# A decoder layer's mixer: masked products in two buffers, and the weighing of a finished group moved behind level 0 and the gate projection

## The chip, the cores and the metric

The kernel runs on one core of a Trainium2 chip. The metric is device time in microseconds of one execution, the median over the runs. Engines are named as in the profile: PE (TensorE, matmuls), PEld (its weight loads), DVE (VectorE), ACT (ScalarE), POOL (GpSimd), SP (SyncE, which issues DMAs).

## The reference

One decoder layer over 32 sequences of 100 tokens with 256 channels, in float32, with three stages, each with a residual: a recurrent mixer, cross attention, and experts. Only the mixer is touched:

```python
def step(S, inp):
    q_t, k_t, v_t, w_t = inp
    kv = k_t[..., :, None] * v_t[..., None, :]
    o_t = jnp.einsum('bhk,bhkv->bhv', q_t, S + u[None, :, :, None] * kv)
    S = jnp.exp(w_t)[..., None] * S + kv
    return (S, o_t)
...
o = (o - mean) / jnp.sqrt(var + EPS)
o = o.reshape(B, T, Hh * V) * gn_weight + gn_bias
o = o * jax.nn.silu(g)
return o @ W_o.T
```

Here q, k, v, w and g are projections of the normalised input mixed with its shifted self, w = -exp(...), and there are 4 heads with keys of 32 and values of 64.

## The kernel before

The mixer (`stage_mixer`) works on 8 groups of 4 sequences. The recurrence is not stepped: for each sequence and head a 100 x 100 matrix of weights between tokens, `attn`, is built in 8 levels. Level 0 gives the diagonal. Levels 1 to 7 give the blocks whose size doubles with each level; between levels q and k are multiplied by decay products (`decay_q`, `decay_k`, L512 and L528). On PE, `level` (L723) multiplies k by `q_heads` into `bank_l`; on ACT, `heads` (L394) lays out `q_heads` for the next level; on DVE, `collect` (L535) copies the products from `bank_l` into `attn` under a mask (L542 for level 0, L562, L554, L555 and L552 for the others). Entries that no mask takes stay zero, from one memset on POOL (L282).

When all levels of a group are collected, PE's `weigh` (L744) multiplies `attn` with the values into the two banks `bank_t`. DVE takes the statistics of each head of the result (`head_stats`, L565, per bank; `head_moments`, L571), POOL the reciprocal root (`head_norm`), DVE centres and scales (`head_scale`, L577), PE turns it (`turn_out`), ACT applies weight and bias, POOL multiplies with the gate, PE projects (`project_out`), and DVE adds to the residual.

Groups overlap: the body for group g does the levels of g, the end of g-1 (from the weighing on) and, with the pieces of `front`, the beginning of g+1 (mixing and projections; piece 7 is g's own gate projection). Each engine runs its own list of such steps in the order in which it is written, with semaphores between engines; there is no planner. Groups 0, 1, 6 and 7 are written out, 2 to 5 are a loop of two turns with two bodies each. On DVE, in a body's step s = 0, stand the first bank's statistics of g-1, the collecting of level 0, the second bank's statistics and the moments; in step 1 `decay_q`, `decay_k`, the collecting of level 1, `head_scale` and the gate. On PE a body begins with the weighing of g-1.

`attn` is one buffer. So the collecting of level 0 of g waits until the weighing of g-1 is done (`o_summed`):

```python
dve.wait_ge(level_summed, g * LEVELS * G + j + 1)
after(dve, o_summed, 2 * g)
```

and `level` lets the second half of level 0 wait for the copies of the first half, since two banks are used in turn.

Of the kernel before, what the change touches and what calls it, by code (L numbers as in the profile page):

```python
# [26 lines left out]
BATCH, T, D = 32, 100, 256  # L27
# [41 lines left out]
def stage_mixer(nc, w, x, x1, slot_rows, out, filled):  # L69
# [9 lines left out]
    with ExitStack() as ctx:  # L79
# [44 lines left out]
        decay = sb("decay", [128, 2, G, TP])  # L124
        total = sb("total", [128, 2, G * TP // 2])
        q_heads = sb("q_heads", [128, 2, RH, G, T])
        attn = sb("attn", [T, G, RH, T])
        val = sb("val", [T, 2, G, D])
        tanh_g = sb("tanh_g", [128, CC, GT])
        half_g = sb("half_g", [128, CC, GT])  # L130
# [126 lines left out]
        def _(pool):  # L257
# [21 lines left out]
            norm(0)  # L279
            pool.memset(q_heads[:, 0], 0.0).then_inc(consts, 1)  # L280
            pool.memset(q_heads[:, 1], 0.0).then_inc(consts, 1)
            pool.memset(attn[:], 0.0).then_inc(consts, 1)  # L282
            pool.memset(total[:], 1.0).then_inc(consts, 1)
            pool.wait_ge(consts, CONSTS)

# [24 lines left out]
            for i in range(BRANCHES):  # L310
                mix(0, i)
            norm(1)

            def body(g, p, more):
                first = isinstance(g, int) and g == 0
# [134 lines left out]
        def _(dve):  # L450
# [81 lines left out]
                dve.tensor_tensor(kv[:, :, 0], kv[:, :, 0], tv[:, :, 1:2].to_broadcast([128, nseg, half]),  # L532
                                  ALU.mult).then_inc(k_decayed, 1)

            def collect(g, lv):  # L535

                if lv == 0:
                    for j in range(G):
                        dve.wait_ge(level_summed, g * LEVELS * G + j + 1)
                        after(dve, o_summed, 2 * g)  # L540
                        dve.sem_inc(waited, 1)
                        dve.copy_predicated(attn[:, j], diagonal[:].unsqueeze(1).to_broadcast([T, RH, T]),  # L542
                                            bank_l[j % 2][0:T, 0:GT].rearrange("p (h t) -> p h t", h=RH)
                                            ).then_inc(attn_done, 1)
                    return
                for i in range(2):
                    dve.wait_ge(level_summed, (g * LEVELS + lv) * G + 2 * i + 2)
                    cols = COLS[lv]
                    src = bank_l[i][0:T, 0:8 * cols].rearrange("p (n c) -> p n c", n=8)
                    dst = attn[:, 2 * i:2 * i + 2].rearrange("p b h t -> p (b h) t")  # L550
                    if lv == LEVELS - 1:
                        dve.tensor_copy(dst[0:64, :, 64:T], src[0:64]).then_inc(attn_done, 1)  # L552
                    elif lv == LEVELS - 2:
                        dve.tensor_copy(dst[0:32, :, 32:64], src[0:32, :, 0:32]).then_inc(attn_done, 1)  # L554
                        dve.tensor_copy(dst[64:96, :, 96:T], src[64:96, :, 32:36]).then_inc(attn_done, 1)  # L555
                    else:
                        half = 1 << (lv - 1)
                        nseg = cols // half
                        to = dst[:, :, 0:nseg * 2 * half].rearrange("p n (s two h) -> p n s two h", two=2, h=half)
                        mask = masks[:, lv - 1, 0:cols].rearrange("p (s h) -> p s h", h=half)  # L560
                        dve.sem_inc(waited, 1)
                        dve.copy_predicated(to[:, :, :, 1], mask.unsqueeze(1).to_broadcast([T, 8, nseg, half]),  # L562
                                            src.rearrange("p n (s h) -> p n s h", h=half)).then_inc(attn_done, 1)
# [43 lines left out]
            def body(g, p, more):  # L607
                first = isinstance(g, int) and g == 0
                for s in range(LEVELS):
                    if s == 5 and two_more(g):  # L610
                        norm_stats(g + 2)
                    if 1 <= s < LEVELS - 1:
                        decay_q(g, p, s + 1)
                        decay_k(g, p, s + 1)
                    if s == 0 and not first:
                        head_stats(g - 1, 0)
                    collect(g, s)
                    if s == 0 and not first:
                        head_stats(g - 1, 1)
                        head_moments(g - 1)  # L620
                    if s == 1 and not first:
                        head_scale(g - 1)
                    if s == 7 and two_more(g):
                        front(g + 2, p, 1)
                    if s == 1 and not first:
                        front(g, p, 7)
                    if more and 1 < s < 7:
                        front(g + 1, 1 - p, s)
                    if 5 <= s <= 6 and not first:
                        residual(g - 1, s - 5)  # L630
# [9 lines left out]
        def _(pe):  # L640
# [103 lines left out]
            def weigh(g, p):  # L744
# [3 lines left out]
                for i in range(2):  # L748
                    for j in (2 * i, 2 * i + 1):
                        for h in range(RH):  # L750
                            mm = pe.matmul(bank_t[i][0:T, (j % 2) * D + h * RV:(j % 2) * D + (h + 1) * RV],
                                           attn[:, j, h, :], val[:, p, j, h * RV:(h + 1) * RV], start=True, stop=True)
                    mm.then_inc(o_summed, 1)

            def turn_out(g):
# [25 lines left out]

            def body(g, p, more):
                first = isinstance(g, int) and g == 0
                if not first:
                    weigh(g - 1, 1 - p)
                for s in range(LEVELS):
                    if s == 0 and not first:
                        level(g, p, 0, (0, 1))
                        front(g, 7)
                        level(g, p, 0, (2, 3))  # L790
                    else:
                        level(g, p, s)
                    if s == 2 and not first:
# [1339 lines left out]
```

## Time and profile before

| what | value |
|---|---|
| median of 3 runs | 1441.59 us |
| lowest and highest | 1439.81 and 1442.03 us |
| the profiled execution | 1454.23 us |
| its span, first to last instruction | 1452.4 us |
| its mean granted TensorE clock | 0.967 |
| mixer, from the start to its last residual add | about 416 us |

The profile is one execution, with its own time; the span is what the instructions cover of it. A timeline row gives the start and the length in us of instructions of the same kind merged into one row, with their count, and in brackets the idle time of the engine before them and what ended it. A PE row counts two passes for each float32 matmul.

### The profile page before, as it was taken

Reading aid. Unit: us, or ns where it says so; the run is one execution under the profiler, and the core shown is the slowest. Engines: PE = TensorE matmul, PEld = TensorE weight load, DVE = VectorE, ACT = ScalarE, POOL = GpSimd, SP = SyncE. Lnnn points to the kernel's source line nnn. Section 1 sums busy time; section 2 is a strip of 40 time slices with the busy share of each in tenths; the row PEclk is TensorE's granted clock in tenths of the full one; section 3 lists DMA queues with packets and bytes.
Section 4 is the critical chain, followed back from the end, with each engine's and each line's share of the span. In section 5 each row is a group of like instructions: output and inputs, shape, how many; then the busy total and the mean of one; then the engine's idle time right before and its main releaser. Section 6 shows DMA issues by size and latency. Waiting matters only on the chain.

```text
span 1452.4 us, 30935 instructions
## 1 busy us (share of the span) xinstructions
PE 1316.8 (91%) x9852; PEld 889.5 (61%) x9853; DVE 934.3 (64%) x1964; ACT 622.5 (43%) x1519; POOL 746.1 (51%) x1080
## 2 busy tenths in 40 slices
PE   5789998999749999999999999999988999999996
PEld 3456655666535666666666666666655566666664
DVE  2587787777614888888888888888884322222221
ACT  2455544554313555555555555555543221211221
POOL 5234443243144678777787777877754322222222
PEclk9999999999757999999999999999999999999998
DMA  4996000000026554545544545545532322222221
GB/s 143 281 318 176 1 1 1 0 1 1 1 64 88 106 118 120 122 123 124 124 101 120 122 124 126 117 121 125 117 85 59 56 45 44 47 45 46 44 44 22
DMA packets 152749, 127.80 MB, mean 88 GB/s; under 512 B 41630, under 2 KB 145510, under 8 KB 152614
## 3 DMA queue, kind: packets, MB, share of 16 engines
q1 hardware_dynamic: 140310, 112.02, 31.3%
q0 software_dynamic: 12304, 14.10, 6.3%
q8 instruction: 71, 1.16, 0.4%
q14 instruction: 64, 0.52, 0.1%
HBM read 35.90 MB, written 44.83 MB: 56 GB/s over the span
## 4 chain that ended last, share of the span: by engine, by line
PE 56%; DVE 8%; issue 3%; ACT 2%; DMA 1%; SPq 0%; another core or an unknown queue 0%; POOL 0%; DVEq 0%; ACTq 0%; POOLq 0%
PE bank_st L1948 10%; PE bank_v L1966 7%; PE bank_s L1780 6%; PE bank_v L1768 6%; PE bank_o L1810 4%; PE bank_st L1790 4%; DVE neg_raw L1469 4%; PE bank_m L1743 4%; PE bank_s L1948 3%; PE bank_m L1832 2%; PE bank_st L1799 2%; DVE bank_st L1480 2%; PE bank_o L1957 2%; PE bank_v L1758 1%; PE bank_m L1820 1%
## 5 line engine op out<-in xcount | busy, mean ns | idle before, releaser
L1469 DVE TENSOR_REDUCE neg_raw<-bank_s 100x2 f32<-100x722 f32 x256 | 229.4, 896 | 32.1 <-PE bank_s L1780 30.2
L1316 ACT ACTIVATE prob<-bank_st 120x400 f32<-120x400 f32 (+1 forms) x384 | 166.2, 513 | 159.4 <-PE bank_st L1799 159.4
L1256 POOL DMA_INDIRECT out<-result,target x57 | 88.4, 1550 | 234.4 <-DVE result L1686 186.0
L1480 DVE TENSOR_SCALAR bank_st<-bank_st 121x1200 f32<-121x1200 f32 x128 | 180.3, 1408 | 1.2 <-PE bank_st L1790 0.8
L1681 DVE TENSOR_TENSOR hidden<-silu,bank_st 128x512 f32<-128x512 f32 x57 | 39.2, 688 | 192.7 <-PE bank_st L1948 192.7
L1948 PE MATMUL bank_st<-expert_w,rows_t 128*128 x344 | 159.3, 599 | 0.7 <-issue 0.5
L409 ACT ACTIVATE q_heads<-q 32x192 f32<-32x192 f32 (+3 forms) x224 | 82.7, 369 | 140.8 <-DVE q L521 136.4
L1780 PE MATMUL bank_s<-k_st,q_st 96*128 96x361 bf16 x512 | 124.1, 324 | 15.5 <-DVE neg_raw L1469 10.1
L1155 POOL TENSOR_TENSOR neg_diag<-xident_b,neg_max 100x400 bf16<-100x400 bf16 x128 | 109.4, 855 | 47.6 <-DVE neg_max L1474 47.0
L741 PE MATMUL bank_l<-q_heads,k 128*100 128x192 f32 (+4 forms) x512 | 114.9, 366 | 18.7 <-ACT q_heads L409 7.3
L293 POOL TENSOR_TENSOR mixed<-part,xn_t 128x400 f32<-128x400 f32 x80 | 84.4, 1080 | 82.0 <-DVE part L462 81.9
L1425 ACT ACTIVATE hidden_t<-bank_o 128x512 f32<-128x512 f32 x57 | 34.0, 597 | 196.5 <-PE bank_o L1957 190.3
L741 PEld LDWEIGHTS bank_l<-q_heads,k 128*100 128x100 f32 x512 | 81.5, 172 | 51.9 <-issue 14.0
L1790 PE MATMUL bank_st<-q_st,k_st 96*128 96x100 bf16 x1536 | 108.6, 209 | 5.0 <-ACT prob L1316 0.6
L1790 PEld LDWEIGHTS bank_st<-q_st,k_st 96*128 96x128 bf16 x1536 | 83.0, 98 | 43.4 <-ACT prob L1316 28.7
L1966 PE MATMUL bank_v<-residual,hidden_t 128*128 x456 | 108.0, 380 | 1.0 <-ACT hidden_t L1425 0.9
L1948 PEld LDWEIGHTS bank_st<-expert_w,rows_t 128*128 128x128 f32 x344 | 63.6, 192 | 71.9 <-issue 71.7
L1743 PE MATMUL bank_m<-kv,xw_k 96*128 96x361 f32 x256 | 93.6, 490 | 10.9 <-DMA kv<-in_ctx_t 10.2
L1768 PE MATMUL bank_v<-xw_v,kv 96*120 96x256 f32 (+1 forms) x384 | 98.5, 394 | 1.4 <-ACT xval L1334 0.7
L1810 PE MATMUL bank_o<-prob,xval 120*32 120x100 f32 (+1 forms) x3072 | 93.7, 255 | 0.0
L1799 PE MATMUL bank_st<-neg_diag,xones_b 100*128 100x400 bf16 x384 | 87.3, 336 | 5.1 <-DVE bank_st L1480 5.1
L1966 PEld LDWEIGHTS bank_v<-residual,hidden_t 128*128 128x128 f32 x456 | 82.3, 190 | 10.8 <-issue 2.0
(231 smaller groups left out, 2545.8 us busy)
## 6 DMA issues: line engine op xcount, KB each, us to landing
k_st<-k_part SPq DMA_DIRECT2D x384, 90.2 KB
slot_rows<-empty SPq DMA_DIRECT2D x9, 2967.0 KB, 26.3
q_st<-q_part SPq DMA_DIRECT2D x192, 50.0 KB
kv<-in_ctx_t SPq DMA_DIRECT2D x32, 270.8 KB
expert_w<-in_w SPq DMA_DIRECT2D x16, 512.0 KB
rows<-slot_rows SPq DMA_DIRECT2D x57, 129.0 KB
residual<-in_w SPq DMA_DIRECT2D x16, 256.0 KB
residual<-in_x SPq DMA_DIRECT2D x8, 400.0 KB
```

The source lines that it names most:

```text
L741: pe.matmul(bank[0:T, at:at + RH * cols], k[:, p, j, 0:T], q_heads[:, lv % 2, :, j, 0:cols], start=True, stop=True).then_inc(level_summed, 1)
L1316: act.activation(prob[0:KEYS[c], t % 2, c], bank_st[0:KEYS[c], c, 0:4 * T], ACT.Exp).then_inc(exp_done, 1)
L1469: dve.tensor_reduce(neg_raw[:, h:h + 2], bank_s[0:T, :, 0:S], AX.X, ALU.max, negate=True).then_inc(max_done, 1)
L1480: dve.tensor_scalar(tile, tile, CLAMP, -CLAMP, ALU.min, ALU.max).then_inc(clipped, 1)
L1743: mm = pe.matmul(bank_m[:, 0:S], w_k[:, i, c * 128:(c + 1) * 128], kv[:, p, i], start=(i == 0), stop=(i == 1))
L1768: mm = pe.matmul(bank_v[0:KEYS[c], (c % 2) * D:(c % 2 + 1) * D], kv[:, p, i, KEY0[c]:KEY0[c] + KEYS[c]], w_v[:, i], start=(i == 0), stop=( ...
L1780: mm = pe.matmul(bank_s[0:WIDE, i, 0:S], q_st[r][:, h * T:h * T + WIDE], k_st[r][:, h * S:(h + 1) * S], start=True, stop=True)
L1790: mm = pe.matmul(bank_st[0:WIDE, c, j * T:(j + 1) * T], k_st[r][:, at:at + WIDE], q_st[r][:, h * T:(h + 1) * T], start=(j == 0), stop=Fals ...
L1799: pe.matmul(bank_st[0:WIDE, c, 0:4 * T], ones_b[:], neg_diag[:, t % 2].rearrange("p j t -> p (j t)"), start=False, stop=True, skip_group_c ...
L1810: mm = pe.matmul(bank_o[32 * j:32 * j + 32, t * T:(t + 1) * T], val[0:KEYS[c], p, c, 17 * (4 * t + j):17 * (4 * t + j) + 32], prob[0:KEYS[ ...
L1948: mm = pe.matmul(dst, rows_t[:, u, c], w1_of[:, bass.ds(expert, 1), c, half * F:(half + 1) * F].rearrange("p o f -> p (o f)"), start=(c == ...
L1966: mm = pe.matmul(ebank_y[:, 0:D], hidden_t[:, u, f], w2_of[:, bass.ds(expert, 1), f].rearrange("p o d -> p (o d)"), start=(f == 0), stop=( ...
```

## The change

`attn` gets a second buffer; the parity p of the group selects it in the collecting and the weighing. POOL zeroes the second buffer later than the first, behind the first group's mixing and the second group's norm; DVE waits for that once, in group 1. The collecting of level 0 now waits for the weighing of g-2. On DVE both banks' statistics stand behind all of the collecting of level 0. On PE the weighing stands behind level 0, whose halves enclose the gate projection.

```diff
-        attn = sb("attn", [T, G, RH, T])
+        attn = sb("attn", [T, 2, G, RH, T])
...
-            pool.memset(attn[:], 0.0).then_inc(consts, 1)
+            pool.memset(attn[:, 0], 0.0).then_inc(consts, 1)
...
             norm(1)
+            pool.memset(attn[:, 1], 0.0).then_inc(consts, 1)
...
-            def collect(g, lv):
+            def collect(g, p, lv, batches=range(G)):
...
-                        after(dve, o_summed, 2 * g)
+                        after(dve, o_summed, 2 * (g - 1))
...
-                        dve.copy_predicated(attn[:, j], diagonal[:].unsqueeze(1).to_broadcast([T, RH, T]),
+                        dve.copy_predicated(attn[:, p, j], diagonal[:].unsqueeze(1).to_broadcast([T, RH, T]),
...
+                    if isinstance(g, int) and g == 1 and s == 0:
+                        dve.wait_ge(consts, CONSTS + 1)
                     if s == 0 and not first:
+                        collect(g, p, 0)
                         head_stats(g - 1, 0)
-                    collect(g, s)
-                    if s == 0 and not first:
                         head_stats(g - 1, 1)
                         head_moments(g - 1)
+                    else:
+                        collect(g, p, s)
...
-                                           attn[:, j, h, :], val[:, p, j, h * RV:(h + 1) * RV], start=True, stop=True)
+                                           attn[:, p, j, h, :], val[:, p, j, h * RV:(h + 1) * RV], start=True, stop=True)
...
-                if not first:
-                    weigh(g - 1, 1 - p)
                 for s in range(LEVELS):
                     if s == 0 and not first:
                         level(g, p, 0, (0, 1))
                         front(g, 7)
                         level(g, p, 0, (2, 3))
+                        weigh(g - 1, 1 - p)
                     else:
                         level(g, p, s)
```

PE at the start of body 1, before. L673 is the turning of the normalised input (the end of the body before), L751 the weighing, L741 the levels (400 columns: level 0; 200: levels 1 and 2), L644 with w_g the gate projection, L680 the first projection of the next group:

```order
L673 MATMUL bank_f<-ident,xn 128x100 x8
L751 MATMUL bank_t<-val,attn 100x64 x16
L741 MATMUL bank_l<-q_heads,k 100x400 x2
L644 MATMUL bank_f<-mixed,w_g 128x400 x4
L741 MATMUL bank_l<-q_heads,k 100x400 x2
L741 MATMUL bank_l<-q_heads,k 100x200 x4
L680 MATMUL bank_f<-xz,w_x 128x400 x4
```

The same place with the change (its lines are numbered 4 higher):

```order
L677 MATMUL bank_f<-ident,xn 128x100 x8
L745 MATMUL bank_l<-q_heads,k 100x400 x2
L648 MATMUL bank_f<-mixed,w_g 128x400 x4
L745 MATMUL bank_l<-q_heads,k 100x400 x2
L755 MATMUL bank_t<-val,attn 100x64 x16
L745 MATMUL bank_l<-q_heads,k 100x200 x4
L684 MATMUL bank_f<-xz,w_x 128x400 x4
```

The 16 matmuls of the weighing have moved from ahead of level 0 to behind it, ahead of level 1.

DVE at the start of body 1, before: L568 the statistics, L542 the collecting of level 0, L575 the moments, L521 to L532 the decays, L562 the collecting of level 1:

```order
L568 BN_STATS gn_stats<-bank_t 100x6 x8
L542 COPY_PREDICATED attn<-diagonal,bank_l 100x400 x4
L568 BN_STATS gn_stats<-bank_t 100x6 x8
L575 BN_AGGR gn_mv<-gn_stats 100x2 x16
L521 TENSOR_TENSOR q<-q,decay 128x256
L525 TENSOR_TENSOR total<-decay 128x256
L532 TENSOR_TENSOR k<-k,decay 128x256
L562 COPY_PREDICATED attn<-masks,bank_l 100x400 x2
```

With the change (lines numbered 1 higher):

```order
L543 COPY_PREDICATED attn<-diagonal,bank_l 100x400 x4
L569 BN_STATS gn_stats<-bank_t 100x6 x16
L576 BN_AGGR gn_mv<-gn_stats 100x2 x16
L522 TENSOR_TENSOR q<-q,decay 128x256
L526 TENSOR_TENSOR total<-decay 128x256
L533 TENSOR_TENSOR k<-k,decay 128x256
L563 COPY_PREDICATED attn<-masks,bank_l 100x400 x2
```

The first 8 statistics have moved behind the four copies; all 16 now stand between the copies and the decays.

## Rows read from the trace of the kernel before

**Rows 1.** The page: busy time, share of the span, instructions of each engine.

```profile
PE 1316.8 (91%) x9852; PEld 889.5 (61%) x9853; DVE 934.3 (64%) x1964; ACT 622.5 (43%) x1519; POOL 746.1 (51%) x1080
```

**Rows 2.** Busy time in a stretch from weighing to weighing; then clock, DMA share, GB/s.

```profile
267.00:311.81 44.81, 41.31 (x197) 28.65 (x195) 35.98 (x99) 23.27 (x54) 17.99 (x18) 1.00 0.00 0
```

**Rows 3.** PE's waits from 86 to 356 us: total us, times, longest.

```profile
PE bank_f L644 <- POOL mixed L293: 8.2, 6, 1.4
PE bank_t L761 <- DVE normed L589: 5.5, 10, 0.9
PE bank_l L741 <- ACT q_heads L409: 4.0, 4, 1.1
PE bank_l L741 <- DVE attn L542: 2.3, 7, 1.1
```

**Rows 4.** Timeline of PE at the boundary of group 6: start, length, line, operation.

```profile
311.81 3.04 PE L751 MATMUL bank_t<-val,attn 100*100 100x64 f32 x32
314.68 1.54 PE L741 MATMUL bank_l<-q_heads,k 128*100 128x400 f32 x4
316.06 2.85 PE L644 MATMUL bank_f<-mixed,w_g 128*128 128x400 f32 x8
318.74 1.51 PE L741 MATMUL bank_l<-q_heads,k 128*100 128x400 f32 x4
320.51 1.57 PE L741 MATMUL bank_l<-q_heads,k 128*100 128x200 f32 x8 [0.26 <-DVE attn L542]
...
325.50 1.73 PE L741 MATMUL bank_l<-q_heads,k 128*100 128x200 f32 x8 [0.74 <-DVE attn L562]
```

**Rows 5.** Timeline of DVE at the same boundary.

```profile
316.47 1.14 DVE L568 BATCH_NORM_STATS2 gn_stats<-bank_t 100x6 f32<-100x64 f32 x8
...
319.76 1.27 DVE L542 COPY_PREDICATED attn<-diagonal,bank_l 100x400 f32<-100x400 int32 x2 [1.16 <-PE bank_l L741]
320.93 1.14 DVE L568 BATCH_NORM_STATS2 gn_stats<-bank_t 100x6 f32<-100x64 f32 x8
...
323.30 0.39 DVE L521 TENSOR_TENSOR q<-q,decay 128x256 f32<-128x256 f32 x1
```

**Rows 6.** Timeline of ACT at the same boundary.

```profile
310.32 0.60 ACT L382 ACTIVATE val<-bank_f 100x512 f32<-100x512 f32 x1 [0.90 <-PE bank_f L651]
310.81 2.57 ACT L409 ACTIVATE q_heads<-q,bonus 32x400 f32<-32x400 f32 x4
```

**Rows 7.** Timeline of ACT at groups 1, 2 and 5.

```profile
85.30 2.56 ACT L409 ACTIVATE q_heads<-q,bonus 32x400 f32<-32x400 f32 x4
...
129.92 2.56 ACT L409 ACTIVATE q_heads<-q,bonus 32x400 f32<-32x400 f32 x4
...
279.00 1.60 ACT L409 ACTIVATE q_heads<-q 32x200 f32<-32x200 f32 x4 [3.96 <-DVE q L521]
```

**Rows 8.** Timeline of PE at groups 1, 2, 5 and 7.

```profile
89.00 1.54 PE L741 MATMUL bank_l<-q_heads,k 128*100 128x400 f32 x4
...
133.96 1.54 PE L741 MATMUL bank_l<-q_heads,k 128*100 128x400 f32 x4
...
280.82 1.60 PE L741 MATMUL bank_l<-q_heads,k 128*100 128x200 f32 x8 [0.92 <-ACT q_heads L409]
...
356.59 3.04 PE L751 MATMUL bank_t<-val,attn 100*100 100x64 f32 x32 [0.54 <-DVE attn L552]
```

**Rows 9.** Timeline of DVE at group 7.

```profile
358.25 1.15 DVE L568 BATCH_NORM_STATS2 gn_stats<-bank_t 100x6 f32<-100x64 f32 x8 [1.72 <-PE bank_t L751]
```

**Rows 10.** Timeline of POOL in the first 65 us.

```profile
12.31 1.43 POOL L282 MEMSET attn<- 100x1600 f32 x1
...
64.30 3.90 POOL L293 TENSOR_TENSOR mixed<-part,xn_t 128x400 f32<-128x400 f32 x4 [17.37 <-DVE part L462]
```

**Rows 11.** Timeline of DVE at group 4, where the loop turns.

```profile
227.33 1.15 DVE L568 BATCH_NORM_STATS2 gn_stats<-bank_t 100x6 f32<-100x64 f32 x8 [1.89 <-issue]
```

**Rows 12.** Timeline of PE: the last group's weighing.

```profile
393.01 4.92 PE L751 MATMUL bank_t<-val,attn 100*100 100x64 f32 x32 [0.71 <-DVE attn L552]
```

More of the change, by code:

```diff
@@ L533, in decay_k @@
                                   ALU.mult).then_inc(k_decayed, 1)
-            def collect(g, lv):
+            def collect(g, p, lv, batches=range(G)):
                 if lv == 0:
-                    for j in range(G):
+                    for j in batches:
                         dve.wait_ge(level_summed, g * LEVELS * G + j + 1)
-                        after(dve, o_summed, 2 * g)
+                        after(dve, o_summed, 2 * (g - 1))
                         dve.sem_inc(waited, 1)
-                        dve.copy_predicated(attn[:, j], diagonal[:].unsqueeze(1).to_broadcast([T, RH, T]),
+                        dve.copy_predicated(attn[:, p, j], diagonal[:].unsqueeze(1).to_broadcast([T, RH, T]),
                                             bank_l[j % 2][0:T, 0:GT].rearrange("p (h t) -> p h t", h=RH)
@@ L549, in collect @@
                     src = bank_l[i][0:T, 0:8 * cols].rearrange("p (n c) -> p n c", n=8)
-                    dst = attn[:, 2 * i:2 * i + 2].rearrange("p b h t -> p (b h) t")
+                    dst = attn[:, p, 2 * i:2 * i + 2].rearrange("p b h t -> p (b h) t")
                     if lv == LEVELS - 1:
```

## The prediction

> **What bounds the kernel now.** I read the page first, then the stretches from one weighing to the next, then PE's waits, then the timelines of PE, ACT and DVE around one boundary between groups. On the page PE is busy for 91% of the span [rows 1], so the naive reading is that only PE's work counts. A stretch from one weighing to the next corrects that: it lasts 44.81 us and PE is busy in 41.31 of them, at a granted clock of 1.00 (its 2.4 GHz level) [rows 2]. PE's idle time in six such stretches is four kinds of wait [rows 3]: for POOL's mixed (8.2), for DVE's normed (5.5), for ACT's heads (4.0) and for the level 0 copy of DVE, L542 (2.3), with a smaller one for L562. All lie in the first half of a group, between the weighing and the projection on w_r; behind that projection PE runs without a wait to the group's end. So a group is a fixed PE run plus a chain across engines, and whatever lengthens that chain lengthens the kernel. The mixer comes before a block boundary, so nothing later takes up its delay.
>
> The chain at the boundary of group 6 (body 6) reads: PE weighs from 311.81, starts level 0 at 314.68, the gate projection at 316.06, the second half of level 0 at 318.74 [rows 4]. DVE takes the first bank's statistics at 316.47, waits 1.16 us for level 0, copies from 319.76, starts the second bank's statistics at 320.93, and reaches decay_q at 323.30 [rows 5]. From decay_q on, level 2's heads, the collecting, normed, part and mixed follow in DVE's order, and all PE waits named above hang on them. **decay_q's start is the clock by which the change is to be judged.**
>
> **What is removed and moved: the start of level 0.** The weighing, 2.87 us of PE (314.68 − 311.81), leaves the place ahead of level 0. Level 0 does not start 2.87 us sooner, because it needs all four heads of ACT. Their activations start at 310.81, straight behind the value copy that started at 310.32, and take 2.57 us: they end at 313.38 [rows 6]. From an ACT head's end to PE's first matmul on it took 0.22 us (279.00 + 1.60 = 280.60, PE at 280.82 [rows 7, 8]). So level 0 starts at 313.60, sooner by 1.08 us, and PE idles from 311.81 to 313.60, a new wait of 1.79 us. At group 1 the same sum gives 85.30 + 2.56 + 0.22 = 88.08 against 89.00, 0.92 sooner; at group 2 129.92 + 2.56 + 0.22 = 132.70 against 133.96, 1.26 sooner [rows 7, 8]. Nothing brings the heads forward: ACT's order is untouched.
>
> **What the move puts on the chain: the weighing before the statistics.** Call level 0's start S. Before, the second statistics started at S + 6.25 (320.93 − 314.68). Now PE issues half of level 0 (1.38, from 314.68 to 316.06), the gate projection (2.68, to 318.74), the other half (1.38) and then the weighing (2.88). That the weighing's last bank is readable 0.22 us after its last issue I take from the last group, where nothing covered it: weighing from 356.59, half of it 1.44, first statistics at 358.25 [rows 8, 9]. The second statistics start at S + 1.38 + 2.68 + 1.38 + 2.88 + 0.22 = S + 8.54: later by 2.29 us against S. The last two level 0 copies do leave DVE sooner: their pair starts 1.02 us behind its half of level 0 (319.76 − 318.74) and takes 1.27, so with S = 313.60 it ends at 313.60 + 4.06 + 1.02 + 1.27 = 319.95. But DVE then stands at the first statistics until the weighing has begun (S + 5.44) and its first bank is readable (1.66 later, 358.25 − 356.59), at 320.70, and again at the second until 322.14. From there to decay_q it is 2.37 us as before (323.30 − 320.93): 324.51 in place of 323.30. Behind it are queued the 16 moments, decay_q, decay_k, level 1's collecting and head_scale, and ACT and POOL wait for those.
>
> **Sum.** 2.29 − 1.08 = 1.21 us a group at group 6; 2.29 − 0.92 = 1.37 at group 1, 2.29 − 1.26 = 1.03 at group 2. Groups 1 to 7 weigh their predecessor in the moved place (the eighth weighing, at the end, is untouched): 7 × 1.21 = **8.5 us**. PE's side agrees in sign: the old waits ahead of level 1 (0.26) and level 2 (0.74 [rows 4]) are swallowed at most in part, against 1.79 us new.
>
> **The other edits.** The second zeroing on POOL costs what the first did, 1.43 us, and lies in the 17.37 us that POOL idles before its mixing at 64.30 [rows 10]; uncovered it would cost 1.43, once. DVE's added wait for it comes in group 1, near 90 us, where the zeroing can start at 46.93 (64.30 − 17.37); I take 0 for a wait already fulfilled, and 0.26, the smallest wait of [rows 4], as its upper end. The copies' wait for the weighing of two groups before is long satisfied, and takes nothing away either, since in the old order PE's queue put the weighing ahead of level 0 anyway: what stalled DVE there was PE's position, not the buffer. No DMA is moved. A code-loading pause can shift: DVE shows one of 1.89 us with no releaser where the loop turns [rows 11]; 0 is my value, −1.89 (it goes) and +3.78 (two more) the ends.
>
> A rule speaks for this change. PE's wait for the level 0 copy comes back at every boundary, 7 waits of 2.3 us in all [rows 3]. The Trainium skill, Perfetto Trace Analysis, Optimization Strategy, says that the same gap repeated on the engine that should be saturated can mean too few buffers. By that rule the second attn buffer would remove those 2.3 us and the kernel would come to about 1439.3; the rows say that the gap belongs to the order, since DVE waited for PE [rows 5].
>
> The profiled execution took 1454.23 us, 12.6 more than the median of 1441.59; the sum gives 1462.7 for such an execution and **1450.1 us** for the median. I carry the 8.5 over unchanged.
>
> **Rivals.**
> 1. *Faster: the heads don't hold level 0.* If the heads were ready when PE is free, level 0 would start 2.87 sooner against 2.29 lost: −0.58 a group, −4.1 in seven, **1437.5 us**. It decides at a head start of 2.29 us: the heads would have to end by about 312.2. For it: only PE's order changes, and PE's order was the binding one. Against it: they ended at 313.38 [rows 6], and the value copy ahead of them waits for PE's own projection, so they move with PE.
> 2. *No change: only PE's order is permuted.* DVE's delay is taken up by waits already there (PE waits 8.2 us in six groups for mixed [rows 3]), or PE's 2.3 us of waits for the level 0 copy go and nothing comes in their place: **1439.3 to 1443 us**. Against: mixed is itself behind DVE's part, in DVE's order behind decay_q.
> 3. *Much slower: the clock falls.* Weighing in the last group took 4.92 us where it takes 3.04 at the full level [rows 4, 12], after PE had idled more: the 1.2 GHz level. If each of the 7 new idles brought such a fall, and each cost these 1.88 us, 13.2 come on top: **1463.3 us**. Against: the waits of up to 1.1 us in these groups left it at 1.00 [rows 2, 3]; 1.79 in one piece is new.
>
> The Trainium skill, TensorE: Matmul & The Clock Gate, A second HAM failure mode, says that short idles between groups of matmuls, frequent enough, make the clock swing between its levels; by it rival 3 would come about.
>
> That the change doesn't do what it says is excluded for the order, by the rows of PE and DVE shown with the change.
>
> **How the numbers follow.** Forecast 0.80, rival 1 0.06, rival 2 0.08, rival 3 0.06. The forecast's own span: seven groups at 1.03 to 1.37 give 7.2 to 9.6; with the pause and a microsecond or so of the last group's changing clock it reaches from 1445 to 1456.5. The range is **1444 to 1456.5**: it leaves out rivals 1 and 3 and most of 2, near 2 in 10. A measurement of this kernel tells about 0.2% (2.9 us) from no change. Faster by more than that: rival 1 and a sliver, 0.07. Within: rival 2 and the forecast's lowest corner, 0.09. Slower: 0.84.
>
> **What would show it.** In the profile after: PE stands idle about 1.8 us before each group's first level 0 matmul, released by ACT's q_heads; the wait for L542 almost goes; DVE waits for bank_t before both statistics of a group; and a stretch from one weighing to the next lasts about 46.0 us instead of 44.8. Wrong: stretches no longer than before (the chain had slack), a PE idle of well under a microsecond ahead of level 0 (the heads came sooner), or a granted clock below 1.00 inside groups 1 to 6.

## The result, and the profile after

The changed kernel takes 1447.05 us in the median of 6 runs (1445.81 to 1452.35), the kernel before 1441.07 us (1439.81 to 1442.25, 6 runs). The ratio is 1.0047, with a 95% interval of 1.0030 to 1.0064: slower by about 6.8 us (4.3 to 9.2 by the interval; the medians differ by 6.0), where 8.5 was predicted.

The span of the profiled execution moved the other way, from 1452.4 to 1447.4 us. That comes from the stages behind the mixer, which the edit doesn't touch: from the mixer's last residual add to the span's end it is 1036.6 us before (1452.4 − 415.8), 1025.6 changed (1447.4 − 421.8), and 1024.5 (1437.7 − 413.2) in the run with only the second buffer below. This part took 1024.5 to 1025.6 us in the profiles of the changed kernel and of the first four runs below, and 1035.7 to 1038.2 in those of the last five, whatever their order in the mixer; the profile of the kernel before belongs with the latter. What makes these 11 us is not known. I therefore compare stretches of the mixer, and times only as ratios to the kernel before, run beside it.

The page, busy time by engine, answers to [rows 1]: nothing has changed in the amounts.

```profile
PE 1316.4 (91%) x9852; PEld 890.1 (61%) x9853; DVE 934.8 (65%) x1964; ACT 620.2 (43%) x1519; POOL 746.1 (52%) x1081
```

The stretch from one weighing to the next (group 5 to group 6) answers to [rows 2]: 45.76 us instead of 44.81 with the same PE work, at the same clock of 1.00.

```profile
279.56:325.32 45.76, 41.21 (x196) 28.81 (x195) 36.18 (x100) 23.24 (x53) 17.97 (x18) 1.00 0.00 1
```

PE's waits from 86 to 360 us, against [rows 3]: the wait for ACT's heads grew from 4.0 to 12.2 us (six new waits ahead of level 0, of 1.48 to 1.67 us, make up 9.5 of them), that for the level 0 copy (now L543) fell from 2.3 to 1.5 and stands at one boundary only, that of group 4, where the loop turns, and those for mixed and normed are as they were.

```profile
PE bank_l L745 <- ACT q_heads L410: 12.2, 10, 1.7
PE bank_f L648 <- POOL mixed L293: 8.2, 6, 1.4
PE bank_t L765 <- DVE normed L590: 5.8, 10, 0.9
PE bank_l L745 <- DVE attn L543: 1.5, 1, 1.5
PE bank_l L745 <- DVE attn L563: 1.1, 2, 0.6
```

PE's timeline at the boundary of group 6 (against [rows 4]). Level 0 starts at 319.86 behind an idle time of 1.48 us; the weighing runs from 325.32 behind level 0's second half.

```profile
317.53 0.85 PE L677 MATMUL bank_f<-ident,xn 100*128 100x100 f32 x8
319.86 1.59 PE L745 MATMUL bank_l<-q_heads,k 128*100 128x400 f32 x4 [1.48 <-ACT q_heads L410]
321.29 2.85 PE L648 MATMUL bank_f<-mixed,w_g 128*128 128x400 f32 x8
323.97 1.51 PE L745 MATMUL bank_l<-q_heads,k 128*100 128x400 f32 x4
325.32 2.96 PE L755 MATMUL bank_t<-val,attn 100*100 100x64 f32 x32
328.11 1.55 PE L745 MATMUL bank_l<-q_heads,k 128*100 128x200 f32 x8
...
332.90 1.73 PE L745 MATMUL bank_l<-q_heads,k 128*100 128x200 f32 x8 [0.55 <-DVE attn L563]
```

ACT at the same boundary (against [rows 6]): the heads start right behind the value copy and end at 319.81. PE starts 0.05 later.

```profile
316.75 0.60 ACT L383 ACTIVATE val<-bank_f 100x512 f32<-100x512 f32 x1 [0.91 <-PE bank_f L655]
317.25 2.56 ACT L410 ACTIVATE q_heads<-q,bonus 32x400 f32<-32x400 f32 x4
```

DVE at the same boundary (against [rows 5]). Both banks' statistics wait for the weighing, 0.64 and 0.27 us, and decay_q starts at 330.69. Decay_k (L533) and the scaling of `normed` (L590) follow.

```profile
324.99 1.27 DVE L543 COPY_PREDICATED attn<-diagonal,bank_l 100x400 f32<-100x400 int32 x2 [1.02 <-PE bank_l L745]
326.90 1.15 DVE L569 BATCH_NORM_STATS2 gn_stats<-bank_t 100x6 f32<-100x64 f32 x8 [0.64 <-PE bank_t L755]
328.31 1.15 DVE L569 BATCH_NORM_STATS2 gn_stats<-bank_t 100x6 f32<-100x64 f32 x8 [0.27 <-PE bank_t L755]
...
330.69 0.39 DVE L522 TENSOR_TENSOR q<-q,decay 128x256 f32<-128x256 f32 x1
...
331.37 0.43 DVE L533 TENSOR_TENSOR k<-k,decay 128x256 f32<-128x256 f32 x1
...
334.69 1.27 DVE L590 TENSOR_TENSOR normed<-normed,gn_rstd 100x512 f32<-100x512 f32 x2
```

To compare the two boundaries, take the end of the body before, E, as zero: the instant at which PE's next instruction could issue. Before, it is the start of the weighing, 311.81. After, the transposes that end the body start at 317.53 and take 0.71 to the next issue, as in the runs below where the weighing still follows them: 318.24. Decay_q then starts at E + 11.49 before (323.30 − 311.81) and at E + 12.45 after (330.69 − 318.24): **0.96 us later, and the stretch is 0.95 us longer** (45.76 − 44.81). Seven groups give 6.7 us.

The body of group 5, read in the same way, gives a little more: decay_q at E + 12.53 (284.93 − 272.40) instead of E + 11.49, and 45.84 us from its E to the next instead of 44.81, thus 1.04 and 1.03. From weighing to weighing it is less, because the wait for the heads is 0.08 us shorter at group 6 than at group 5. Seven times 1.03 is 7.2. The ratio allows 4.3 to 9.2 us, so it tells neither of these sums from the forecast of 8.5; only the stretches do, and that 6.7 comes so close to 6.8 is chance.

### The profile page after: what moved, and what is told of

It reads as the page before. It is cut to its first block, busy times and chain, and to the rows that moved or that the text cites. A ratio compares the mean times of both kernels' runs of the same rounds, so it can differ in the third digit from the quotient of the medians.

```text
span 1447.4 us, 30930 instructions
## 1 busy us (share of the span) xinstructions
PE 1316.4 (91%) x9852; PEld 890.1 (61%) x9853; DVE 934.8 (65%) x1964; ACT 620.2 (43%) x1519; POOL 746.1 (52%) x1081
## 3 DMA queue, kind: packets, MB, share of 16 engines
q8 instruction: 71, 1.16, 0.4%
## 4 chain that ended last, share of the span: by engine, by line
PE 61%; issue 3%; ACT 3%; DVE 3%; DMA 1%; SPq 0%; POOL 0%; ACTq 0%; DVEq 0%; POOLq 0%
PE bank_st L1951 10%; PE bank_v L1969 7%; PE bank_v L1771 6%; PE bank_s L1783 6%; PE bank_st L1793 6%; PE bank_m L1746 6%; PE bank_o L1813 5%; PE bank_s L1951 3%; PE bank_st L1802 3%; PE bank_m L1835 2%; PE bank_o L1960 2%; PE bank_v L1761 1%; DVE neg_raw L1472 1%; PE bank_m L1823 1%; ACT heads_t L1332 1%
## 5 line engine op out<-in xcount | busy, mean ns | idle before, releaser
L1793 PE MATMUL bank_st<-q_st,k_st 96*128 96x100 bf16 x1536 | 113.4, 209 | 5.7 <-ACT prob L1319 0.6
```

What stands on the lines that cost most here:

```text
L1793: mm = pe.matmul(bank_st[0:WIDE, c, j * T:(j + 1) * T], k_st[r][:, at:at + WIDE], q_st[r][:, h * T:(h + 1) * T], start=(j == 0), stop=Fals ...
```

## The experiments

Times are ratios to the kernel before, which took 1441.1 us beside the first four runs, 1453.9 beside the next three and 1453.0 beside the last two. Beside each stands the stretch from the weighing of group 5's body to that of group 6's (44.81 before, 45.76 changed). Edits are shown against the kernel named.

**The second buffer alone** (against the changed kernel: PE's and DVE's old order).

```diff
+                if not first:
+                    weigh(g - 1, 1 - p)
...
                         level(g, p, 0, (2, 3))
-                        weigh(g - 1, 1 - p)
...
                     if s == 0 and not first:
-                        collect(g, p, 0)
                         head_stats(g - 1, 0)
+                    collect(g, p, s)
+                    if s == 0 and not first:
                         head_stats(g - 1, 1)
                         head_moments(g - 1)
-                    else:
-                        collect(g, p, s)
```

> Two attn buffers, with PE and DVE in the order of the kernel before. Theory A (the order alone acts; a group's pace is set by when DVE reaches decay_q): ratio to the kernel before 1.000, within 0.001, and 44.8 us from weighing to weighing. Theory B (the one buffer made PE's repeated wait for the level 0 copy): PE's 2.3 us of waits for that copy go, ratio 0.998, 44.5 us a stretch.

Measured: ratio 0.9998 (0.9989 to 1.0007), and a stretch of 44.80 us:

```profile
266.70:311.50 44.80, 41.31 (x196) 28.64 (x194) 35.97 (x99) 23.26 (x54) 17.98 (x18) 1.00 0.00 0
```

PE's waits for the level 0 copy add up to 2.2 us there, against 2.3. The buffer does nothing by itself, and its zeroing costs nothing that shows. Theory B falls: its 0.998 lies outside the interval.

**DVE's new order alone** (against the changed kernel: the weighing back at the start of PE's body).

```diff
+                if not first:
+                    weigh(g - 1, 1 - p)
...
                         level(g, p, 0, (2, 3))
-                        weigh(g - 1, 1 - p)
```

> Two buffers and DVE's new order (all level 0 copies, then both banks' statistics), with the weighing left ahead of level 0 on PE. Theory A: the first bank's statistics (1.06 us) no longer lie in DVE's wait for level 0's second half, so decay_q comes 1.06 us later: 45.9 us a stretch, +7.4 us in seven groups, ratio 1.005, about all that the whole change costs. Rival C (PE's moved weighing is the cause): ratio 1.000 and 44.8 us.

Measured: ratio 1.0044 (1.0031 to 1.0058), 45.85 us a stretch. DVE's timeline at group 6 shows the mechanism: its wait for level 0's second half grows from 1.16 to 2.23 us, since the first statistics no longer fill it, and all 16 statistics stand behind.

```profile
325.71 1.27 DVE L543 COPY_PREDICATED attn<-diagonal,bank_l 100x400 f32<-100x400 int32 x2 [2.23 <-PE bank_l L745]
326.87 2.19 DVE L569 BATCH_NORM_STATS2 gn_stats<-bank_t 100x6 f32<-100x64 f32 x16
...
330.29 0.40 DVE L522 TENSOR_TENSOR q<-q,decay 128x256 f32<-128x256 f32 x1
```

Decay_q at E + 12.54 (330.29 − 317.75). So DVE's reordering alone (on top of the second buffer, which does nothing) costs what the whole change costs. With PE's part of the change two further terms come in that cancel: level 0 starts sooner, and the statistics wait for the weighing.

**The changed kernel with short heads** (in groups 1 to 7 only the first token of each sequence is laid out for level 0, so the kernel leaves out the rest of the diagonal).

```diff
-                    if lv == 0:
+                    if lv == 0 and not (isinstance(g, int) and g == 0):
+                        src, dst = q[rows, p, :, 0:1], q_heads[rows, 0, h, :, 0:1]
+                    elif lv == 0:
                         src, dst = q[rows, p, :, 0:T], q_heads[rows, 0, h]
```

> The changed kernel, where ACT lays out only the first token of each sequence for level 0 in groups 1 to 7 (the diagonal of the others is left out of the computation, with the same number of instructions and semaphores). Theory A: ACT's four level 0 heads shrink from 2.57 us to about 1 and PE's idle of 1.6 us ahead of level 0 goes almost wholly: some 1.4 us less a stretch than the changed kernel, 44.3 us, ratio to before 0.997. If something else held level 0: 45.8 us and 1.005.

Measured: ratio 0.9982 (0.9973 to 0.9991), 44.46 us. ACT's four heads take 1.25 us instead of 2.56, so the saving was 1.31, less than I had guessed. PE, at group 6, waits 0.17 us for them instead of 1.48:

```profile
310.88 1.59 PE L747 MATMUL bank_l<-q_heads,k 128*100 128x400 f32 x4 [0.17 <-ACT q_heads L412]
```

The stretch shrinks by 1.30 us, one for one with the heads.

**The kernel before with the same short heads**, the control (same edit).

> The kernel before with the same shortened level 0 heads, the control. Theory A: the weighing covers the heads there, so nothing changes: 44.8 us, ratio 1.000 within 0.001. Rival (shorter heads help by themselves, by way of ACT's copy of xn_t and DVE's delta behind them): up to 1.4 us a stretch, ratio 0.993.

Measured: ratio 0.9996 (0.9987 to 1.0005), 44.81 us. DVE's delta does come 1.3 us sooner there, and DVE then waits 2.48 us for level 0's second half instead of 1.16. Shorter heads are worth nothing as long as the weighing covers them; moving it uncovered them. The two runs together also show rival 1's condition: with the heads nearly out of the way the changed order beats the old one, by 2.6 us against the kernel before and by 2.0 against this control (0.9982 against 0.9996).

**The weighing in halves** (against the changed kernel).

```diff
+                if not first:
+                    weigh(g - 1, 1 - p, (0,))
...
                         level(g, p, 0, (0, 1))
-                        front(g, 7)
+                        weigh(g - 1, 1 - p, (1,))
+                        front(g, 7, (0,))
                         level(g, p, 0, (2, 3))
-                        weigh(g - 1, 1 - p)
+                        front(g, 7, (1,))
...
                     if s == 0 and not first:
-                        collect(g, p, 0)
+                        collect(g, p, 0, (0, 1))
                         head_stats(g - 1, 0)
+                        collect(g, p, 0, (2, 3))
                         head_stats(g - 1, 1)
```

> Two buffers. PE: first half of the weighing, first half of level 0, second half of the weighing, first half of the gate projection, second half of level 0, second half of the gate projection. DVE: first two level 0 copies, first bank's statistics, last two copies, second bank's statistics. Theory A: one half of the weighing (1.44 us) lies in PE's wait for the heads (1.6 us), and level 0's second half starts 5.8 us behind the end of the body before instead of 6.9 (before) or 7.1 (changed): decay_q about 1.05 us sooner than before, 43.75 us a stretch, ratio 0.995. If decay_q did not set the pace (PE's work did): 44.8 us, ratio 1.000.

Measured: ratio 0.9952 (0.9938 to 0.9965), 43.77 us. PE does not wait for the heads, and level 0's second half starts at E + 5.83 (311.86 − 306.03):

```profile
306.03 1.62 PE L758 MATMUL bank_t<-val,attn 100*100 100x64 f32 x16
307.65 1.59 PE L748 MATMUL bank_l<-q_heads,k 128*100 128x400 f32 x4
309.08 1.55 PE L758 MATMUL bank_t<-val,attn 100*100 100x64 f32 x16
310.46 1.56 PE L649 MATMUL bank_f<-mixed,w_g 128*128 128x400 f32 x4
311.86 1.51 PE L748 MATMUL bank_l<-q_heads,k 128*100 128x400 f32 x4
```

DVE reaches decay_q at 316.40, E + 10.37, that is 1.12 us sooner than before.

**The weighing between the halves of level 0, the gate projection behind both** (against the changed kernel; DVE as in the run just told).

```diff
                         level(g, p, 0, (0, 1))
-                        front(g, 7)
+                        weigh(g - 1, 1 - p)
                         level(g, p, 0, (2, 3))
-                        weigh(g - 1, 1 - p)
+                        front(g, 7)
```

> Two buffers. PE: first half of level 0, the whole weighing, second half of level 0, gate projection; DVE as in the run with halves. PE keeps its wait of 1.6 us for the heads. Theory A: level 0's second half starts 5.9 us behind the end of the body before, the statistics wait for nothing, decay_q is 1.0 us sooner than before: ratio 0.995, 43.8 us, although PE idles ahead of level 0. A theory that PE's new idle by itself is the cost: slower than before, ratio 1.003 or more.

Measured: ratio 0.9984 (0.9969 to 0.9999), 44.09 us: 0.72 us less a stretch, not 1.0, so the size was missed and the sign was right. From E to E a body is 0.64 us shorter, 4.5 in seven, which is the edge of what the ratio allows (0.1 to 4.5 us). Decay_q does come at E + 10.41 (319.43 − 309.02, with E from the transposes at 308.31 and 0.71), 1.08 sooner than before. But level 1 now follows the gate projection, and decay_k, the instruction behind decay_q and total, must wait for level 1:

```profile
319.43 0.39 DVE L522 TENSOR_TENSOR q<-q,decay 128x256 f32<-128x256 f32 x1
...
320.47 0.43 DVE L533 TENSOR_TENSOR k<-k,decay 128x256 f32<-128x256 f32 x1 [0.28 <-PE bank_l L746]
```

This takes back 0.36 us (decay_k 1.04 behind decay_q, 0.68 in the changed kernel). PE idles as long ahead of level 0 as in the changed kernel and the time is still below that of before: PE's new idle is not a cost by itself, only by what it delays.

**decay_q ahead of the statistics** (against the changed kernel).

```diff
                         decay_q(g, p, s + 1)
+                        if s == 1 and not first:
+                            head_stats(g - 1, 0)
+                            head_stats(g - 1, 1)
+                            head_moments(g - 1)
                         decay_k(g, p, s + 1)
...
-                    if s == 0 and not first:
-                        collect(g, p, 0)
-                        head_stats(g - 1, 0)
-                        head_stats(g - 1, 1)
-                        head_moments(g - 1)
-                    else:
-                        collect(g, p, s)
+                    collect(g, p, s)
```

> The changed kernel with DVE's decay_q and total for level 2 ahead of the two statistics instead of behind the moments. Theory A: these 0.7 us of work fill DVE's waits for the weighing (0.64 and 0.27 us at each boundary), nothing else moves: 0.7 us less a stretch than the changed kernel, 45.1 us, ratio to before 1.0015. If DVE's waits for the weighing are not on the path: 45.8 us, ratio 1.0045.

Measured: ratio 1.0024 (1.0015 to 1.0033), 45.29 us: 0.47 us less than the changed kernel, not 0.7. The wait for the first bank is gone, that for the second still there:

```profile
322.55 0.41 DVE L522 TENSOR_TENSOR q<-q,decay 128x256 f32<-128x256 f32 x1
...
323.29 1.15 DVE L569 BATCH_NORM_STATS2 gn_stats<-bank_t 100x6 f32<-100x64 f32 x8
324.70 1.15 DVE L569 BATCH_NORM_STATS2 gn_stats<-bank_t 100x6 f32<-100x64 f32 x8 [0.27 <-PE bank_t L753]
...
327.08 0.39 DVE L533 TENSOR_TENSOR k<-k,decay 128x256 f32<-128x256 f32 x1
...
330.58 1.29 DVE L590 TENSOR_TENSOR normed<-normed,gn_rstd 100x512 f32<-100x512 f32 x2
```

```profile
327.63 2.91 POOL L301 TENSOR_TENSOR gn_rstd<-gn_rstd,power 100x16 f32<-100x16 f32 x1
```

I had let 0.7 us of work fill both waits, but the second one opens only after the first bank's statistics, where no work was put. Of the first wait's 0.64 us, 0.47 came back. Decay_k did come 0.68 us sooner than in the changed kernel (E + 12.45 against E + 13.13, with E = 313.92 + 0.71). But the moments came no sooner, POOL's reciprocal root made from them ends at 330.54, and L590 starts at 330.58: E + 15.95 against E + 16.45, 0.50 sooner. So a second branch, from the moments over POOL to L590, took up the rest.

The run shows more than it was made for. Decay_q came at E + 7.92, 3.57 us sooner than in the kernel before, and still a stretch is 0.48 us longer than there.

**The gate projection in halves** (against the kernel before: one buffer, the whole weighing first; on DVE the first two level 0 copies now stand ahead of the first bank's statistics).

```diff
                         level(g, p, 0, (0, 1))
-                        front(g, 7)
+                        front(g, 7, (0,))
                         level(g, p, 0, (2, 3))
+                        front(g, 7, (1,))
...
                     if s == 0 and not first:
-                        head_stats(g - 1, 0)
-                    collect(g, s)
-                    if s == 0 and not first:
+                        collect(g, 0, (0, 1))
+                        head_stats(g - 1, 0)
+                        collect(g, 0, (2, 3))
                         head_stats(g - 1, 1)
                         head_moments(g - 1)
+                    else:
+                        collect(g, s)
```

> One attn buffer and the whole weighing first, as in the kernel before; only the gate projection is cut in halves, with level 0's second half between them, and DVE takes two level 0 copies, the first bank's statistics, two copies, the second bank's statistics. Theory A: what the run with halves gained came from level 0's second half starting sooner (5.6 us behind the end of the body before, against 6.9), not from the second buffer or the split weighing: 43.7 us a stretch, ratio 0.995. If the buffer or the split weighing made the gain: 44.8 us, ratio 1.000.

Measured: ratio 0.9923 (0.9908 to 0.9938), 43.45 us. It beats both kernels, with one buffer and the weighing whole, so neither the second buffer nor the split weighing made the gain. Level 0's second half starts at E + 5.59 and DVE waits for nothing on the way to decay_q at E + 10.14 (315.68 − 305.54), 1.35 us sooner than before; the stretch is 1.36 shorter.

```profile
305.54 3.04 PE L755 MATMUL bank_t<-val,attn 100*100 100x64 f32 x32
308.42 1.54 PE L745 MATMUL bank_l<-q_heads,k 128*100 128x400 f32 x4
309.79 1.51 PE L646 MATMUL bank_f<-mixed,w_g 128*128 128x400 f32 x4
311.13 1.51 PE L745 MATMUL bank_l<-q_heads,k 128*100 128x400 f32 x4
```

```profile
311.17 1.13 DVE L568 BATCH_NORM_STATS2 gn_stats<-bank_t 100x6 f32<-100x64 f32 x8
312.22 1.21 DVE L542 COPY_PREDICATED attn<-diagonal,bank_l 100x400 f32<-100x400 int32 x2
313.32 1.13 DVE L568 BATCH_NORM_STATS2 gn_stats<-bank_t 100x6 f32<-100x64 f32 x8
...
315.68 0.39 DVE L521 TENSOR_TENSOR q<-q,decay 128x256 f32<-128x256 f32 x1
```

Seven groups at 1.36 are 9.5 us; the ratio gives 11.2 (0.0077 of some 1453), and its interval reaches from 9.0 to 13.4. PE's order and DVE's were changed together, and no run has one without the other. An estimate from the rows of the kernel before: DVE would be ready for the second pair of copies at E + 6.79 in its old order (319.76 − 1.16 − 311.81), and they would be readable at E + 6.61 (5.59, and the 1.02 from issue to copy), so PE's cut alone should remove the wait of 1.16 us.

**And xn_t sooner on ACT** (against the run before).

```diff
                     elif more:
-                        heads(g + 1, 1 - p, 0)
+                        heads(g + 1, 1 - p, 0, (0, 1) if two_more(g) else range(RH))
...
                         front(g + 2, p, 0)
+                        heads(g + 1, 1 - p, 0, (2, 3))
...
                     if s == 0 and not first:
-                        collect(g, 0, (0, 1))
                         head_stats(g - 1, 0)
-                        collect(g, 0, (2, 3))
                         head_stats(g - 1, 1)
+                        collect(g, 0, (0, 1))
                         head_moments(g - 1)
+                        collect(g, 0, (2, 3))
```

> As the run before it, and ACT makes xn_t after two of the four level 0 heads instead of after all four, so that DVE's delta and xz come 1.3 us sooner; DVE takes both statistics ahead of the level 0 copies and the moments between the second and third copy. The heads end at most 2.5 us behind the end of the body before, still under the weighing's 2.87. Theory A: the statistics and moments fill DVE's waits, decay_q comes 3.5 us sooner than before, decay_k then waits for level 1, and the parts come 2.0 us sooner: 42.8 us a stretch, ratio 0.990. If PE's own work already bounds a group after the run before: no further gain, 43.7 us, ratio 0.995.

Measured: ratio 0.9925 (0.9912 to 0.9939), which is not told apart from the run before; the stretch is 43.05 us, 0.40 shorter, where 0.9 was expected. Decay_q came at E + 8.44 (311.32 − 302.88), 3.05 us sooner than in the kernel before. Then decay_k waits:

```profile
311.32 0.40 DVE L522 TENSOR_TENSOR q<-q,decay 128x256 f32<-128x256 f32 x1
...
313.36 0.43 DVE L533 TENSOR_TENSOR k<-k,decay 128x256 f32<-128x256 f32 x1 [1.29 <-PE bank_l L746]
```

and PE waits anew for the level 0 copy (4.0 us in six boundaries, 2.2 of them where the loop turns), since the statistics now stand ahead of it. What follows on DVE now hangs on level 1, and so on PE's own order. Why the 0.40 us a stretch don't show in the whole time isn't settled; by seven groups they would be 2.8 us, 0.2%, at the edge of what these intervals can tell. Against the kernel before there is no conflict: seven times 1.76 is 12.3 us, and the ratio allows 8.9 to 12.8.

## Why the prediction was right, and where it was off

The time lies in the range, the direction was given 0.84, and the size is 8.5 us forecast against 6.8 measured (4.3 to 9.2). A group was forecast at 1.21 us and measured at 0.95 to 1.03. The sum was sound; what it made of its two halves was not, as the end of this section tells.

- **The chain as the bound.** Right: in every run the stretch moved with DVE's part of the chain, whatever happened to PE's idle. But "decay_q's start is the clock" was too early a point of it. It holds only while decay_k and `normed` follow at a fixed distance. In two runs decay_k waited for level 1, and with decay_q first `normed` waited for POOL. The table gives the body of group 5 in each run, all from its E: the starts of decay_q, of decay_k and of the scaling of `normed` (L589 in the kernel before, L590 in the changed one, the same step in the others), and the time to the next E. The start of the scaling follows that time within 0.03 us in all of them, decay_q's doesn't.

| run | decay_q | decay_k | scaling | E to E |
|---|---|---|---|---|
| before | 11.49 | 12.16 | 15.48 | 44.81 |
| changed | 12.53 | 13.21 | 16.52 | 45.84 |
| DVE's order alone | 12.53 | 13.21 | 16.53 | 45.85 |
| changed, short heads | 11.22 | 11.90 | 15.21 | 44.54 |
| weighing in halves | 10.45 | 11.12 | 14.45 | 43.76 |
| weighing inside level 0 | 10.49 | 11.53 | 14.84 | 44.17 |
| decay_q first | 7.99 | 12.53 | 16.03 | 45.36 |
| gate projection in halves | 10.14 | 10.81 | 14.15 | 43.45 |
| and xn_t sooner | 8.45 | 10.42 | 13.73 | 43.05 |

- **Heads hold level 0.** Right, and shown by the pair with short heads: 1.31 us less heads gave 1.30 us in the changed order and nothing in the old. The term was mis-sized by the start-up: I took 0.22 us from a head's end to PE's first matmul, from a row of level 2. At level 0 it was 0.05 (319.86 − 319.81). The new idle is 1.62 us from E to level 0's start rather than 1.79 (319.86 − 318.24; the row's own 1.48 starts at the modelled end of PE's matmuls).
- **The statistics behind the weighing.** S + 8.54 was forecast, S + 8.45 measured (328.31 − 319.86): the first bank was readable 1.58 us behind the weighing's start (I had 1.66) and the second 2.99 (I had 3.10). These 0.09 and the 0.17 of the heads are the 0.26 us by which 1.21 became 0.95 at group 6. From there to decay_q it took 2.38 against 2.37.
- **The sum over seven groups.** 7 × 0.95 is 6.7. The spread from 1.03 to 1.37 wasn't there: from E to E groups 1, 2, 3 and 5 are 1.11, 0.98, 1.05 and 1.03 us longer, and group 4, with the pause told next, 1.40.
- **The other edits.** The zeroing runs at 45.86 us, behind the second group's norm, in 1.43 us; the buffer as a whole measured 0.9998. The pause that the prediction calls code loading (what it is no run shows) stayed single, at the same place, and grew from 1.89 to 2.16 us. The group that holds it is longer than its neighbours by 1.5 us before (46.30 from E to E) and by 1.9 changed (47.70), so the term taken as 0 was about 0.4, in one profile of each:

```profile
45.86 1.43 POOL L313 MEMSET attn<- 100x1600 f32 x1
```

```profile
231.59 1.08 DVE L543 COPY_PREDICATED attn<-diagonal,bank_l 100x400 f32<-100x400 int32 x2 [2.16 <-issue]
```

- **The rule on repeated gaps** (the Trainium skill, Perfetto Trace Analysis, Optimization Strategy: they can mean too few buffers), as the prediction applied it, gave −2.3 us for the second buffer. With the buffer alone nothing came (0.9989 to 1.0007, where −2.3 us would be 0.9984). The gap went with one buffer, in the run with the gate projection in halves: its seven waits became one, of 1.6 us where the loop turns. It was a matter of order.
- **Rival 1** (heads not held) had the mechanism right and its condition was unmet. When a run met it, the gain was 2.6 us, by way of −0.35 us a stretch (44.46 against 44.81), not −0.58: with the offsets as measured the two terms give 2.20 − 2.87 = −0.67 if level 0 starts at E, and it started 0.32 us behind it (310.88 against 309.85 + 0.71), still released by the heads. **Rival 2** falls with the ratio's interval. **Rival 3**: the clock stayed at 1.00 through groups 1 to 6 of the changed kernel; the fall at every boundary that it needs did not come. Its mechanism is real all the same: it came once in the run with decay_q first, at group 7, and cost 1.66 us there, near the 1.88 of its price (last section).

What the diff as a whole did: its DVE part costs 1.04 to 1.06 us a group by taking the first bank's statistics out of a wait that they filled. Its PE part is worth next to nothing on top. Against the run with DVE's order alone the second pair of copies starts 1.21 us sooner (E + 6.75 against E + 7.96), because level 0 does; the waits for the weighing and the pieces that they split give 0.75 us back ahead of the first bank's statistics and 0.37 behind, which leaves 0.09 at group 6 (decay_q at E + 12.45 against E + 12.54) and nothing at group 5 (E + 12.53 in both). A weighing that covered PE's wait for the heads was exchanged for one that DVE waits for.

This the prediction had wrong. It charged all of the 2.29 us to the weighing that now stands ahead of the statistics, and had no term for DVE's own reordering, though [rows 5] held it: the first bank's statistics, about 1.06 us, lay in front of a wait of 1.16 and made it that short. Its sum came out near because it follows the changed order to the end, and with DVE's new order the place of the weighing hardly matters: 45.84 us a body with it moved, 45.85 with it in the old place. That the terms of PE's move cancel so closely is chance, and from the sum alone one would blame that move. It has no run of its own, nor could it have one: with the first statistics still ahead of the copies, they would wait for a weighing that stands behind level 0's second half, which waits for these copies.

## What to carry to other kernels

Before moving work off the front of a queue, ask what it covers: here 2.87 us of PE work lay on 1.6 us of waiting for another engine, and only the difference could be won. Ask the same of each instruction moved back behind a wait: DVE's first statistics had filled one, and moving them cost a microsecond by itself. When two engines hand work back and forth, look for the half of an instruction group that the other engine waits for, and move only what stands ahead of it: cutting the gate projection in two, with DVE's order fitted to it, won 1.36 us a group where the change lost 0.95. Judge a change to a chain at a point behind which all its branches have met (here the scaling of `normed`), not at the first instruction that comes sooner. A repeated gap is a buffer's fault only if the buffer's wait is the one that ends last, and a run with the buffer alone settles that cheaply.

## What was not expected of the hardware

In the run with DVE's order alone the granted clock was 0.96, not 1.00, over two stretches, those of groups 3 and 5. The latter:

```profile
271.90:317.75 45.85, 42.71 (x197) 29.79 (x195) 35.96 (x99) 23.23 (x54) 17.98 (x18) 0.96 0.00 0
```

There PE had idled 1.97 us in one piece, and the level 2 matmuls behind it took 2.55 us instead of the 1.59 to 1.73 of its rows at the full level. From 288 to 290 us the granted clock was 0.50, the lower level of 1.2 GHz; from 291 us it was 1.00 again.

```profile
286.76 2.55 PE L745 MATMUL bank_l<-q_heads,k 128*100 128x200 f32 x8 [1.97 <-ACT q_heads L410]
```

PE then waited less for mixed (0.98 us instead of the 1.40 of the kernel before), and the stretch was as long as the next one at a clock of 1.00 (45.85 and 45.84), so the fall cost next to nothing there.

It was not so in the run with decay_q first. Ahead of group 7's level 0 PE idled 2.16 us, the granted clock fell to 0.50 from 363 to 365 us, and level 0's first half and the gate projection, behind which DVE waits for level 0's second half, took 2.10 and 4.08 us instead of 1.59 and 2.85. The stretch is 46.95 us instead of 45.29.

```profile
361.51 2.10 PE L743 MATMUL bank_l<-q_heads,k 128*100 128x400 f32 x4 [2.16 <-ACT q_heads L410]
363.40 4.08 PE L646 MATMUL bank_f<-mixed,w_g 128*128 128x400 f32 x8
```

The changed kernel has the same idle at the same place, and its clock stayed at 1.00:

```profile
365.61 1.59 PE L745 MATMUL bank_l<-q_heads,k 128*100 128x400 f32 x4 [2.16 <-ACT q_heads L410]
```

In the run with DVE's order alone, too, idles of 2.14 and 2.05 us brought no fall where 1.98 and 1.97 did. So in these traces an idle of about 2 us was followed by the fall at times, even within one run, and those of up to 1.8 us in groups 1 to 6 never were. What it costs depends on whether a wait behind it takes it up.

The last group's weighing ran at the lower level for the most part in the profile of the kernel before, 4.92 us [rows 12], and took 3.04 in the changed one,

```profile
401.53 3.04 PE L755 MATMUL bank_t<-val,attn 100*100 100x64 f32 x32 [0.71 <-DVE attn L553]
```

but 3.04 also in the run with the second buffer alone, which has the order of before, and in all the others. So this low clock belongs to the execution, not to the order, and can add or hide some 2 us in a single profile. This is why the ends of the mixer in single profiles (415.8 us before, 421.8 changed, 413.2 with the buffer alone) should be read less than the stretches.
